# A new hand-written order of the engines' lists in three residual convolution steps

## The reference

```python
for _ in range(N_STEPS):                              # 3 steps
    t = relu(conv(x, w1) + b1)                        # 3x3, 64 -> 64 channels, SAME
    x = x + H_STEP * (conv(t, w2) + b2)               # H_STEP = 1/3
out = relu(x)
```

## Time and profile before

| | us |
|---|---|
| median of 3 runs (lowest to highest) | 1152.56 (1150.67 to 1153.24) |
| the profiled execution's own time | 1151.02 |
| its span | 1149.2 |
| TensorE busy (PE) | 1076.2, 94% |
| VectorE busy (DVE) | 1044.5, 91% |
| ScalarE busy (ACT) | 652.1, 57% |
| GpSimd busy (POOL) | 506.8, 44% |

### The profile page before, as it was taken

The page is one execution under the profiler, slowest core; times in us unless marked ns, Lnnn a source line. Parts: engine busy times, 40 slices in busy tenths (PEclk is TensorE's granted clock), DMA queues, the critical chain, the costliest instruction groups (busy, mean ns, idle before and its releaser), DMA issues. The chain is left out here.

```text
span 1149.2 us, 20990 instructions
## 1 busy us (share of the span) xinstructions
PE 1076.2 (94%) x7238; PEld 603.5 (53%) x7238; DVE 1044.5 (91%) x1481; ACT 652.1 (57%) x1525; POOL 506.8 (44%) x416
## 2 busy tenths in 40 slices
PE   3269999999999999999978999999999999999996
PEld 3156777777877777778743333333333333333331
DVE  5459999999999999999967999999999999999996
ACT  4567889888888888888632233252233332342332
POOL 5134555445544554455314345344344444444340
PEclk9999999999999999999997999999999999999998
DMA  8110111111111111110000000030000200030003
GB/s 305 48 36 20 38 36 32 29 38 38 29 30 38 38 29 36 32 38 12 19 19 1 1 1 1 1 74 2 1 1 16 58 1 1 1 74 1 1 1 74
DMA packets 87544, 35.83 MB, mean 31 GB/s; under 512 B 70209, under 2 KB 86850, under 8 KB 86930
## 3 DMA queue, kind: packets, MB, share of 16 engines
q1 hardware_dynamic: 85634, 33.81, 11.0%
q10 hardware_dynamic: 1040, 0.35, 0.2%
q0 software_dynamic: 768, 0.33, 0.1%
HBM read 26.09 MB, written 8.39 MB: 30 GB/s over the span
## 5 line engine op out<-in xcount | busy, mean ns | idle before, releaser
L1082 PE MATMUL acc<-mixed,cwp 128*128 128x512 f32 x768 | 355.4, 608 | 4.4 <-DVE mixed L1143 2.9
L1100 ACT ACTIVATE y<-acc,cols 128x1024 f32<-128x1024 f32 x96 | 110.3, 1209 | 271.9 <-PE acc L1092 271.9
L1082 PEld LDWEIGHTS acc<-mixed,cwp 128*128 128x128 f32 x768 | 139.9, 191 | 218.6 <-issue 202.2
L1092 PE MATMUL acc<-mixed,cwp 64*64 64x512 f32 x1536 | 184.2, 600 | 0.0
L842 POOL TENSOR_TENSOR rstd<-var,half 128x8 f32<-128x8 f32 x32 | 80.7, 2522 | 216.8 <-DVE var L733 216.8
L522 DVE TENSOR_TENSOR prod<-qkv 128x1024 f32<-128x1024 f32 x128 | 155.6, 1219 | 7.6 <-POOL qkv L738 7.3
L532 DVE TENSOR_TENSOR prod<-attn,qkv 128x1024 f32<-128x1024 f32 x128 | 155.1, 1236 | 1.1
L1142 POOL TENSOR_TENSOR mixed<-xs 128x256 f32<-128x256 f32 x92 | 74.1, 806 | 159.9 <-DVE xs L1131 159.9
L1108 DVE TENSOR_TENSOR y<-y,acc 128x512 f32<-128x512 f32 x192 | 119.9, 681 | 18.0 <-ACT y L1100 17.8
L564 PE MATMUL cb<-consts,prod 128*128 128x128 f32 x1024 | 133.3, 279 | 0.0
L1116 DVE TENSOR_TENSOR y<-y,acc 128x512 f32<-128x512 f32 x192 | 124.4, 685 | 8.8 <-PE acc L1092 6.4
(11 more groups left out here) (172 smaller groups left out, 1537.8 us busy)
## 6 DMA issues: line engine op xcount, KB each, us to landing
xs<-in_x SPq DMA_DIRECT2D x4, 2048.0 KB, 16.4
xa<-in_x SPq DMA_DIRECT2D x32, 256.0 KB, 2.7
xr<-in_x SPq DMA_DIRECT2D x64, 128.0 KB, 2.9
out_y<-xs SPq DMA_DIRECT2D x32, 256.0 KB, 4.6
cw<-in_L_conv_w POOLq DMA_DIRECT2D x2, 144.0 KB, 3.9
consts<-in_consts ACTq DMA_DIRECT2D x1, 192.0 KB
group<-in_consts SPq DMA_DIRECT2D x1, 64.0 KB
w1n<-in_L_conv_w ACTq DMA_DIRECT2D x1, 64.0 KB
```

The source lines that it names most:

```text
L1082: pe.matmul(psum[PSUM_PAIR[v, q, j]][i][:, :, :], weights(v, i, j).rearrange("p n o -> p (n o)"), mixed[v][i][:, s0:s0 + WIDE, j, :], star ...
L1092: m = pe.matmul(psum[PSUM_PAIR[v, q, j]][i][out, :, :], edge_weights(v, i, j)[rows, :], mixed[v][i][rows, s0 + near:s0 + near + WIDE, j, : ...
L1100: act.activation(pairs(y[i][q][:, :, :]), m1, ACT.Identity, bias=cols[:, (6, 8)[v]:(7, 9)[v]]).then_inc(m1_out[i][q], 1)
```

## The change

It writes the four lists anew, with the same calls, and numbers the accumulators anew. TensorE: in half (1,1) the third product comes ahead of the corners; (0,1) starts with product 3; several corner pairs are swapped; and the list is cut behind the first two products of (1,0). The wait ahead of the first of these is now for the sums, and ahead of the second for m1. ScalarE, VectorE and GpSimd: cut at other places and partly reordered; GpSimd needs no third part, and the loop runs COUNT + 1 times. The function bodies, the lists ahead of the first iteration and SyncE's list are the same.

```diff
--- before.py
+++ after.py
@@ -1022,9 +1022,9 @@
         NW, NC = 2, 4
         COUNT = B // 2 * STEPS
         PSUM_PAIR = {
-            (0, 0, 0): 3, (0, 0, 1): 2, (0, 0, 2): 0, (0, 0, 3): 1, (0, 1, 0): 3, (0, 1, 1): 2, (0, 1, 2): 0,
-            (0, 1, 3): 1, (1, 0, 0): 3, (1, 0, 1): 2, (1, 0, 2): 0, (1, 0, 3): 1, (1, 1, 0): 2, (1, 1, 1): 3,
-            (1, 1, 2): 0, (1, 1, 3): 1
+            (0, 0, 0): 1, (0, 0, 1): 0, (0, 0, 2): 2, (0, 0, 3): 3, (0, 1, 0): 1, (0, 1, 1): 0, (0, 1, 2): 3,
+            (0, 1, 3): 2, (1, 0, 0): 1, (1, 0, 1): 0, (1, 0, 2): 2, (1, 0, 3): 3, (1, 1, 0): 0, (1, 1, 1): 1,
+            (1, 1, 2): 2, (1, 1, 3): 3
         }
 
         xs, cols = top["xs"], top["cols"]
@@ -1162,13 +1162,6 @@
 
         def pe_iteration(pe, g, steps):
             if steps[1]:
-                pe_edges(pe, g - 1, 0, 1, 0)
-                wait(pe, m1_out[0][1], turn(g - 1, 0))
-                wait(pe, m1_out[1][1], turn(g - 1, 0))
-                pe_products(pe, g - 1, 1, 0, 2)
-                wait(pe, sums_done[0][1], turn(g - 1, 0))
-                wait(pe, sums_done[1][1], turn(g - 1, 0))
-                pe_products(pe, g - 1, 1, 0, 3)
                 wait(pe, y_done[0][1][1], turn(g - 1, 0))
                 wait(pe, y_done[1][1][1], turn(g - 1, 0))
                 pe_products(pe, g - 1, 1, 0, 1)
@@ -1177,24 +1170,24 @@
                 wait(pe, y_done[0][1][0], turn(g - 1, 0))
                 wait(pe, y_done[1][1][0], turn(g - 1, 0))
                 pe_products(pe, g - 1, 1, 0, 0)
+                pe_edges(pe, g - 1, 1, 0, 0)
                 pe_edges(pe, g - 1, 1, 0, 1)
-                pe_edges(pe, g - 1, 1, 0, 0)
                 wait(pe, m1_out[0][0], turn(g - 1, 1))
                 wait(pe, m1_out[1][0], turn(g - 1, 1))
                 pe_products(pe, g - 1, 1, 1, 2)
                 wait(pe, sums_done[0][0], turn(g - 1, 1))
                 wait(pe, sums_done[1][0], turn(g - 1, 1))
                 pe_products(pe, g - 1, 1, 1, 3)
-                pe_edges(pe, g - 1, 1, 1, 3)
-                pe_edges(pe, g - 1, 1, 1, 2)
                 wait(pe, y_done[0][0][1], turn(g - 1, 1))
                 wait(pe, y_done[1][0][1], turn(g - 1, 1))
                 pe_products(pe, g - 1, 1, 1, 0)
+                pe_edges(pe, g - 1, 1, 1, 2)
+                pe_edges(pe, g - 1, 1, 1, 3)
                 wait(pe, y_done[0][0][0], turn(g - 1, 1))
                 wait(pe, y_done[1][0][0], turn(g - 1, 1))
                 pe_products(pe, g - 1, 1, 1, 1)
+                pe_edges(pe, g - 1, 1, 1, 1)
                 pe_edges(pe, g - 1, 1, 1, 0)
-                pe_edges(pe, g - 1, 1, 1, 1)
             if steps[0]:
                 wait(pe, m1_out[0][1], turn(g - 1, 1))
                 wait(pe, m1_out[1][1], turn(g - 1, 1))
@@ -1210,16 +1203,16 @@
                 pe_products(pe, g, 0, 0, 0)
                 pe_edges(pe, g, 0, 0, 2)
                 pe_edges(pe, g, 0, 0, 3)
+                pe_edges(pe, g, 0, 0, 1)
                 pe_edges(pe, g, 0, 0, 0)
-                pe_edges(pe, g, 0, 0, 1)
                 wait(pe, m1_out[0][0], turn(g, 0))
                 wait(pe, m1_out[1][0], turn(g, 0))
-                pe_products(pe, g, 0, 1, 2)
+                pe_products(pe, g, 0, 1, 3)
                 wait(pe, sums_done[0][0], turn(g, 0))
                 wait(pe, sums_done[1][0], turn(g, 0))
-                pe_products(pe, g, 0, 1, 3)
+                pe_products(pe, g, 0, 1, 2)
+                pe_edges(pe, g, 0, 1, 3)
                 pe_edges(pe, g, 0, 1, 2)
-                pe_edges(pe, g, 0, 1, 3)
                 wait(pe, y_done[0][0][1], turn(g, 0))
                 wait(pe, y_done[1][0][1], turn(g, 0))
                 pe_products(pe, g, 0, 1, 1)
@@ -1227,26 +1220,33 @@
                 wait(pe, y_done[1][0][0], turn(g, 0))
                 pe_products(pe, g, 0, 1, 0)
                 pe_edges(pe, g, 0, 1, 1)
+                pe_edges(pe, g, 0, 1, 0)
+                wait(pe, sums_done[0][1], turn(g, 0))
+                wait(pe, sums_done[1][1], turn(g, 0))
+                pe_products(pe, g, 1, 0, 2)
+                wait(pe, m1_out[0][1], turn(g, 0))
+                wait(pe, m1_out[1][1], turn(g, 0))
+                pe_products(pe, g, 1, 0, 3)
 
         def act_iteration(act, g, steps):
             if steps[1]:
-                act_hidden(act, g - 1, 0, 1)
-                act_hidden(act, g - 1, 0, 0)
-                act_hidden(act, g - 1, 1, 1)
-                act_hidden(act, g - 1, 1, 0)
-                act_m1(act, g - 1, 0, 0, 1)
-                act_m1(act, g - 1, 0, 1, 1)
-                act_hidden(act, g - 1, 1, 3)
-                act_hidden(act, g - 1, 1, 2)
-                act_hidden(act, g - 1, 0, 2)
-                act_hidden(act, g - 1, 0, 3)
                 act_m1(act, g - 1, 1, 0, 0)
-                act_m1(act, g - 1, 1, 1, 0)
                 act_m1(act, g - 1, 1, 0, 1)
                 act_m1(act, g - 1, 1, 1, 1)
             if steps[0]:
                 act_m1(act, g, 0, 1, 0)
                 act_m1(act, g, 0, 0, 0)
+                act_hidden(act, g, 0, 0)
+                act_hidden(act, g, 0, 1)
+                act_hidden(act, g, 1, 0)
+                act_hidden(act, g, 1, 1)
+                act_m1(act, g, 0, 1, 1)
+                act_m1(act, g, 0, 0, 1)
+                act_hidden(act, g, 1, 3)
+                act_hidden(act, g, 1, 2)
+                act_hidden(act, g, 0, 2)
+                act_hidden(act, g, 0, 3)
+                act_m1(act, g, 1, 1, 0)
             if steps[1]:
                 act_result(act, g - 1, 0, 0)
                 act_result(act, g - 1, 1, 0)
@@ -1255,71 +1255,71 @@
 
         def dve_iteration(dve, g, steps):
             if steps[1]:
-                mix_h(dve, g - 1, 0, 0, inner)
-                dve_sums(dve, g - 1, 0, 0, 1)
-                mix_h(dve, g - 1, 1, 0, outer)
-                dve_sums(dve, g - 1, 0, 1, 1)
-                dve_y(dve, g - 1, 0, 1, 1, 1)
-                dve_y(dve, g - 1, 0, 1, 1, 0)
-                dve_y(dve, g - 1, 0, 0, 1, 1)
-                mix_h(dve, g - 1, 1, 1, outer)
-                dve_y(dve, g - 1, 0, 0, 1, 0)
+                mix_h(dve, g - 1, 0, 2, inner)
                 mix_h(dve, g - 1, 1, 3, outer)
-                mix_h(dve, g - 1, 0, 2, inner)
                 mix_h(dve, g - 1, 0, 2, outer)
-                mix_h(dve, g - 1, 1, 2, outer)
                 mix_h(dve, g - 1, 0, 3, outer)
                 mix_h(dve, g - 1, 0, 3, inner)
+                dve_sums(dve, g - 1, 1, 1, 0)
                 dve_sums(dve, g - 1, 1, 0, 0)
-                dve_sums(dve, g - 1, 1, 1, 0)
+                dve_y(dve, g - 1, 1, 0, 0, 0)
                 dve_y(dve, g - 1, 1, 0, 0, 1)
-                dve_y(dve, g - 1, 1, 0, 0, 0)
                 dve_x(dve, g - 1, 0, 0)
                 dve_y(dve, g - 1, 1, 1, 0, 0)
                 dve_y(dve, g - 1, 1, 1, 0, 1)
+                mix_x(dve, g - 1, 0, 1, outer)
+                dve_x(dve, g - 1, 1, 0)
                 mix_x(dve, g - 1, 0, 0, outer)
-                dve_x(dve, g - 1, 1, 0)
                 mix_x(dve, g - 1, 1, 0, outer)
                 mix_x(dve, g - 1, 1, 1, outer)
...
             if steps[0]:
                 dve_sums(dve, g, 0, 1, 0)
                 dve_sums(dve, g, 0, 0, 0)
+                dve_y(dve, g, 0, 0, 0, 0)
                 dve_y(dve, g, 0, 0, 0, 1)
-                dve_y(dve, g, 0, 0, 0, 0)
                 dve_y(dve, g, 0, 1, 0, 0)
                 dve_y(dve, g, 0, 1, 0, 1)
+                mix_h(dve, g, 0, 0, outer)
                 mix_h(dve, g, 0, 1, inner)
+                mix_h(dve, g, 0, 0, inner)
+                mix_h(dve, g, 1, 0, outer)
+                dve_sums(dve, g, 0, 1, 1)
                 mix_h(dve, g, 0, 1, outer)
-                mix_h(dve, g, 0, 0, outer)
+                dve_sums(dve, g, 0, 0, 1)
+                dve_y(dve, g, 0, 1, 1, 1)
+                dve_y(dve, g, 0, 1, 1, 0)
+                mix_h(dve, g, 1, 1, outer)
+                dve_y(dve, g, 0, 0, 1, 0)
+                dve_y(dve, g, 0, 0, 1, 1)
+                mix_h(dve, g, 1, 2, outer)
...
@@ -1332,8 +1332,8 @@
 
         def run(eng, iteration):
 
-            for g in range(COUNT + 3 - 1):
-                iteration(eng, g, [0 <= g - s < COUNT for s in range(3)])
+            for g in range(COUNT + 2 - 1):
+                iteration(eng, g, [0 <= g - s < COUNT for s in range(2)])
 
         block = ctx.enter_context(nc.Block())
 
```

More of the change, by code:

```diff
@@ L1285, in dve_iteration @@
                 dve_sums(dve, g - 1, 1, 1, 1)
-                mix_x(dve, g - 1, 0, 1, outer)
+                dve_y(dve, g - 1, 1, 0, 1, 1)
                 dve_y(dve, g - 1, 1, 0, 1, 0)
-                dve_y(dve, g - 1, 1, 0, 1, 1)
                 dve_x(dve, g - 1, 0, 1)
@@ L1292, in dve_iteration @@
                 dve_x(dve, g - 1, 1, 1)
+                mix_x(dve, g - 1, 0, 3, outer)
+                mix_x(dve, g - 1, 0, 2, outer)
```

(27 more changed lines are left out.)

## The result

The changed kernel takes 1163.25 us (median of 4 runs, 1162.16 to 1164.15), the one before 1151.62 in 4 runs: a ratio of 1.0099 (95% interval 1.0086 to 1.0112). The forecast was 1162.5 us, in a range from 1158.5 to 1167. The profiled execution took 1164.01 us, its span is 1162.2.

A forecast was written before the change was run, and what follows sets the result against it. TensorE was taken as the bound, within 0.1 us of its order's 43.7 us floor. 1151.0 + 10.1 + 0.5 - 0.2 = 1161.4 us, or 1162.9 from the median, stated as 1162.5; range 1158.5 to 1167.

The forecast's parts named there:

- (c): ScalarE's four result passes delay the second m1; TensorE waits 1.66 us at P(1,1,2), 1.71 at P(1,1,0), three times: +10.1 us.
- The runs (no gain, no loss): TensorE keeps seven pairs of product and corner runs an iteration, so the floor stays 43.7 us: gain 0.
- (a): TensorE's product P(1,0,2) now waits for VectorE's sums of (0,1), expected 0.1 us before it asks: cost 0.
- the rival's 0.95 a half: VectorE's inner mix halves last as long as GpSimd's pass; P(1,0,2) 0.8 us late in 12 iterations: +9.4 us, chance 0.04.
- (b): P(1,1,0), now third in its run, has a weight load waiting for VectorE's y: 0.05 us per plain iteration, 0.5 us.
- The 0.07 us at the corners of (0,0): Lower bound of (b): the whole loss that a 43.77 us iteration shows over the floor goes, -0.07 us each.
- The sum: Profiled 1151.0 us + 10.1 + 0.5 - 0.2 = 1161.4; from the median 1152.56 it gives 1162.9, stated as 1162.5.
- Result passes were not absorbed: Rival at P(1,1,2) in iterations 3, 6 and 9: passes cost no wait, time 1152.5 plus 0.3 us, chance 0.04.
- the granted clock stayed at 1.00 through both waits: Rival: TensorE's clock falls to its lower level in the waits, up to 5 us three times: 1177 us, chance 0.03.

The follow-up runs named there:

- e3_old_order_misplaced: The kernel before, order untouched, with only its four result passes moved between the two m1 of (1, half 0): 1159.35 us, ratio 1.0066.

## Why the prediction was right

*The place of the result passes (c).* Right in mechanism and size. The passes came at 29.36 from the iteration's start (forecast 29.33), the second m1 ended at 34.29 (34.33), P(1,1,2) started at 34.34 (34.42) and the load of P(1,1,0) came at 39.53 (39.48). The iteration took 47.11 (47.1). VectorE stood idle 3.35 us, where I had 3.7. The two runs that moved only these passes give back all but 0.1 us of it. The step was put as two waits at two named products; e3_old_order_misplaced shows the more general form, idle time of an engine with little to spare: by the named products it would have cost 1.66 us there, and it cost 2.62.

*The runs (no gain, no loss).* Right: 14 runs in the order listed, and the kernel with six pairs takes 43.35 us an iteration, 0.42 less, where the earlier trace rows gave 0.37 for a pair.

*P(1,0,2), (a).* Off by a little: 0.12 us each, where I had 0 with 0.1 us to spare. The sums started at 18.67, not 18.50. VectorE's timeline in the changed kernel shows which term was too small:

```profile
807.19 0.69 DVE L1136 TENSOR_TENSOR mixed<-h 128x512 f32<-128x512 f32 x1
...
808.13 0.86 DVE L1143 TENSOR_TENSOR mixed<-h 128x256 f32<-128x256 f32 x1
808.91 0.83 DVE L1142 TENSOR_TENSOR mixed<-h 128x256 f32<-128x256 f32 x1
809.67 0.84 DVE L1143 TENSOR_TENSOR mixed<-h 128x256 f32<-128x256 f32 x1
810.43 1.10 DVE L1136 TENSOR_TENSOR mixed<-h 128x512 f32<-128x512 f32 x1
811.45 1.27 DVE L1108 TENSOR_TENSOR y<-y,acc 128x512 f32<-128x512 f32 x2
```

GpSimd's timeline at the same time:

```profile
808.66 0.80 POOL L1143 TENSOR_TENSOR mixed<-h 128x256 f32<-128x256 f32 x1
809.42 0.80 POOL L1142 TENSOR_TENSOR mixed<-h 128x256 f32<-128x256 f32 x1
810.19 0.79 POOL L1143 TENSOR_TENSOR mixed<-h 128x256 f32<-128x256 f32 x1
```

The halves step 0.76 to 0.78 us apart, as taken, but the outer mix took 1.02 us to the sums instead of 0.82. The 0.82 was half of two outer mixes, and the first of those began at 802.70, ahead of GpSimd's start at 802.92.

Both engines go in step here, one instruction of each every 0.76 us. Beside GpSimd, VectorE's inner half takes 0.42 us more than alone (0.76 for 0.34), and its outer mix too (1.02 for the 0.60 from 807.19). A GpSimd half takes 0.58 us to the next beside VectorE's sums (790.55 to 791.13). The Trainium skill (SBUF — State Buffer, "SBUF: two separate sides") states that one of the two blocks the other for a whole instruction. The trace agrees only in part: the two do take turns, but whole instructions one behind the other would make 0.34 + 0.58 = 0.92 us as an estimate, and the trace has 0.76. The measurement decides, and the rival's 0.95 a half was too long.

*P(1,1,0) in plain iterations, (b).* Right in size: the run of 12 takes 5.41 us where the one at (1,0) takes 5.34 (814.58 to 819.92). TensorE's timeline:

```profile
825.59 5.48 PE L1082 MATMUL acc<-mixed,cwp 128*128 128x512 f32 x12
831.00 1.95 PE L1092 MATMUL acc<-mixed,cwp 64*64 64x512 f32 x16
```

The 0.07 us at the corners of (0,0) went, which I had only as a bound: P(0,0) takes 7.07 us to the corners (792.78 to 799.85), 7.13 in the earlier trace rows. It makes up for (b), so what a plain iteration loses, 0.12 us, is (a), which the sum had at 0.

*The sum.* It added 10.4 us; the convolutions took 10.85 more and the medians lie 11.6 apart. That the forecast came within 0.8 us of the median is in part luck: its base, 1152.56, was the median of three runs that came out at 1151.62 with a fourth, and executions of one kernel differ by some 2 us (last section).

*The rivals.* Result passes were not absorbed; the mixes lasted 0.17 us longer, not 0.9; the granted clock stayed at 1.00 through both waits.

## What to carry to other kernels

Work that comes only in some iterations belongs in a steady-state order too: here four passes of one iteration in three, one call too early in a list taken in order, cost 10 us, and one call later nothing. Look at what the first call behind such work releases, and at the slack of the engine that waits for it: 3.4 us of VectorE's time was lost at a place where it had next to none to spare. When TensorE shows no waits, count its changes between two kinds of weights; here one pair of runs less was worth 0.42 us in 43.77, once the mixes were shared out anew.

## What the runs showed of the hardware that was not expected

The part ahead of the convolutions is the same in both kernels, but the granted clock in it isn't the same in every execution. Busy time and granted clock (us, TensorE busy, clock, DMA share, GB/s) in the profiled execution before:

```profile
60.00:80.00 20.00, 14.41 (x97) 1.00 0.05 14
80.00:100.00 20.00, 16.77 (x163) 1.00 0.11 27
```

And in the one after:

```profile
60.00:80.00 20.00, 13.56 (x84) 0.85 0.05 14
80.00:100.00 20.00, 18.02 (x150) 0.89 0.11 27
```

In the second execution the granted clock was 0.76 from 72 to 76 us and 0.50, the lower level (1.2 GHz for 2.4), from 76 to 84; ahead of that TensorE had stood idle for 2.31 us up to 73.32, where it stood 1.31 in the first. The same eight matmuls (L553) take 2.08 us at 74.42 and 78.31 in the second, and 1.13 at 74.59 and 77.53 in the first. At 60 us the second execution is 0.17 us ahead, at 100 us it is 1.74 behind, and 1.6 of that is left at the first corners. A caution for reading such rows: up to 66 us these matmuls take 2.08 us in both executions, although the granted clock is given as 1.00 there.

The four executions of the changed kernel fall into two pairs, 1162.2 and 1162.5 us at a mean clock of 0.989 and 0.990, and 1164.0 and 1164.2 at 0.984 and 0.985. So a difference of some 1.7 us between two executions can come from a part that an edit does not touch. What decides between the two was not tried.
